# The end of a joined loop: linear products of groups 6 and 7 placed ahead of the first two key tiles, key and value weight halves cast one round earlier

## What is computed

```python
    x = x + _L0_attn_ref(_layernorm(x, axis=-1), ...)      # gated linear attention
    x = x + _L0_ffn_ref(_layernorm(x, axis=-1), ...)       # x2 and w2 rounded to a 6-bit grid, out = xd @ wd.T + bias
    x = x + _L1_xattn_ref(_layernorm(x, axis=-1), ctx_1024, ctx_1024, ...)
    # in _L1_xattn_ref, 16 heads of 32 features:
    q = _split_heads(query @ Wq + bq)
    k = _split_heads(key @ Wk + bk)
    v = _split_heads(value @ Wv + bv)
```

## Time and profile before

| | us |
|---|---|
| median of 3 runs | 1305.11 |
| lowest and highest | 1301.33, 1306.03 |
| the profiled execution | 1304.07 |
| its span | 1302.80 |
| TensorE busy | 1230.7 |
| VectorE busy | 728.5 |
| ScalarE busy | 520.5 |
| GpSimd busy | 141.2 |

### The profile page before, as it was taken

How to read it: one execution, slowest core, us unless ns; L and a number is a source line. 1 busy time by engine, 2 the same in 40 slices (tenths; PEclk the granted TensorE clock), 3 DMA queues, 4 the chain that set the end, 5 groups by cost and what they waited for, 6 DMA issues and landing times. The chain is left out here.

```text
span 1302.8 us, 25903 instructions
## 1 busy us (share of the span) xinstructions
PE 1230.7 (94%) x11069; PEld 917.0 (70%) x11069; DVE 728.5 (56%) x1602; ACT 520.5 (40%) x1032; POOL 141.2 (11%) x163
## 2 busy tenths in 40 slices
PE   6999889989959999999999999999899999999999
PEld 4565467855536777777777777776788767887887
DVE  5368386638884555454545555555585745434342
ACT  3234437543112355445444545454454332222321
POOL 2300022145540300000000000000031100000000
PEclk9999999889989999999999999999899999999999
DMA  9659600200203021000001000001400201011100
GB/s 297 255 203 398 240 1 1 73 1 1 98 17 126 36 98 35 34 34 34 34 34 34 34 34 34 34 34 34 83 1 1 73 1 33 33 33 33 65 33 33
DMA packets 49334, 88.23 MB, mean 68 GB/s; under 512 B 19210, under 2 KB 20284, under 8 KB 45124
## 3 DMA queue, kind: packets, MB, share of 16 engines
q1 hardware_dynamic: 48160, 86.01, 19.3%
q10 hardware_dynamic: 1060, 0.56, 0.2%
HBM read 65.59 MB, written 20.97 MB: 66 GB/s over the span
## 5 line engine op out<-in xcount | busy, mean ns | idle before, releaser
L1941 ACT ACTIVATE W<-W,low 128x512 f32<-128x512 f32 x128 | 91.0, 713 | 58.1 <-DVE low L1858 58.1
L1926 ACT ACTIVATE K<-bank,vecT 128x512 f32<-128x512 f32 x64 | 43.7, 688 | 166.1 <-PE bank L285 166.1
L222 POOL TENSOR_TENSOR rstd<-rstd,half_pow 128x1 f32<-128x1 f32 x48 | 31.8, 664 | 715.0 <-DVE rstd L218 715.0
L285 PE MATMUL bank<-ctxT,Wkv 128*128 128x512 f32 x384 | 96.0, 403 | 10.7 <-DVE ctxT L302 10.7
L1836 DVE TENSOR_TENSOR W<-bank,vecT 128x256 f32<-128x256 f32 x16 | 6.8, 424 | 167.2 <-PE bank L1747 167.2
L1858 DVE CUSTOM_DVE_ANT_0 W<-bank,W 128x512 f32<-128x512 f32 x128 | 80.8, 687 | 31.5 <-PE bank L1726 31.5
L285 PE MATMUL bank<-xT,wT 128*128 128x512 f32 x384 | 94.8, 396 | 0.8 <-ACT W L2764 0.5
L285 PE MATMUL bank<-woT,hR 128*128 128x512 f32 x384 | 93.2, 398 | 2.3 <-DVE woT L302 2.3
L285 PE MATMUL bank<-Wkv,Wq 128*128 128x512 f32 x384 | 93.8, 399 | 0.0
L285 PE MATMUL bank<-Wq,Wkv 128*128 128x512 f32 x384 | 93.0, 394 | 0.0
L285 PE MATMUL bank<-Wkv,ctxT 128*128 128x512 f32 x384 | 92.9, 394 | 0.0
(11 more groups left out here) (345 smaller groups left out, 2232.1 us busy)
## 6 DMA issues: line engine op xcount, KB each, us to landing
W<-ctx_turned SPq DMA_DIRECT2D x16, 1024.0 KB, 4.8
W<-in_ctx_dram SPq DMA_DIRECT2D x8, 1024.0 KB, 10.2
ctx_turned<-ctxT SPq DMA_DIRECT2D x8, 1024.0 KB, 7.6
ctx_turned<-W SPq DMA_DIRECT2D x8, 1024.0 KB, 6.7
XT<-in_ctx_dram SPq DMA_DIRECT2D x4, 1024.0 KB, 11.3
XT<-in_L_ffn_wi_dram SPq DMA_DIRECT2D x4, 1024.0 KB, 6.1
XT<-in_L_ffn_wo_dram SPq DMA_DIRECT2D x4, 1024.0 KB, 5.1
raw_own<-in_ctx_dram SPq DMA_DIRECT2D x3, 1024.0 KB, 11.2
```

The lines of the kernel that those rows point to most:

```text
L222: pool.tensor_tensor(rstd[:, g:g + 1], rstd[:, g:g + 1], half_pow[:], ALU.pow).then_inc(rstd_ok.s, 1)
L285: ins = pe.matmul(dst, stationary(x, k), moving(y, k), start=(first and n == 0), stop=(last and n == len(passes) - 1), skip_group_check=True)
L1926: act.activation(K[:, m, :], bank[:, n % 4, :], ACT.Identity, bias=pcol("L1_xattn_bk", m)).then_inc(ring_a.s, 1)
L1941: act.activation(PR[:, j, :], PR[:, j, :], ACT.Exp, bias=low[:, j:j + 1], scale=-1.0, accum_out=total[:, j:j + 1]).then_inc(expd.s, 1)
```

## The change

On TensorE, key tile 0 leaves round 12 and key tile 1 leaves its place ahead of the linear product of group 7. Both now stand at the end of round 13, behind that product. The waits for the sums of groups 6 and 7 in front of key tiles 2 and 3 become one wait for the sum of group 7 in front of the first transpose of the next stage. On ScalarE and VectorE, the key and value weight halves are made in rounds 1 to 4 in place of 2 to 5. No instruction is added or removed but the one wait.

```diff
@@ -1213,8 +1213,6 @@
                     if 1 <= t <= G:
                         mean_of_pe(t - 1)
-                    if t in (G + 4, G + 5):
-                        key_pe(t - G - 4)
                     if 6 <= t:
                         linear_pe(t - 6)
@@ -1223,6 +1221,9 @@
                     if 1 <= t <= G:
                         variance_pe(t - 1)
+                    if t == G + 5:
+                        for m in range(2):
+                            key_pe(m)
@@ -1410,8 +1411,8 @@
-                    if 2 <= t < C + 2:
-                        key_weights_v(t - 2)
+                    if 1 <= t <= C:
+                        key_weights_v(t - 1)
@@ -1577,8 +1578,8 @@
-                    if 2 <= t < C + 2:
-                        key_weights_a(t - 2)
+                    if t <= C:
+                        key_weights_a(t - 1)
@@ -1766,6 +1767,7 @@
             def tensor():
+                pe.wait_ge(xsum.s, xsum(nth("xsum", 2, G - 1)))
                 for g in range(G):
@@ -1773,7 +1775,6 @@
                     transpose_rows(xn, 3, g, 4 + g % 3)
                     if g in (2, 5):
-                        pe.wait_ge(xsum.s, xsum(nth("xsum", 2, 6 + g // 3)))
                         keys_pe(0, 2 + g // 3)
```

## The result

The changed kernel takes 1297.30 us (median of 20 runs, 1289.72 to 1305.05), the kernel before 1304.96 (20 runs, 1299.51 to 1311.16). The ratio is 0.9948, 95% interval 0.9931 to 0.9964, so the change is worth 6.8 us of 1305, with 4.7 to 9.0 in the interval; the medians are 7.7 apart. The profiled execution took 1300.68 us with a span of 1299.4.

A forecast was written before the change was run, and what follows sets the result against it. The prediction took TensorE, busy for 94% of the span, to bound the kernel. Its terms, 8.5 + 0.8 + 0.75 - 2.0 = 8.05 us off 1305.11, gave 1297.1 us, range 1293.6 to 1302.

The forecast's parts named there:

- Part 1, the order: Rounds 12 and 13 on TensorE: two linear products and one turn fill the 10.3 us idle time, gaining 8.5 us.
- the waits for half_x: On TensorE in front of transposes 3 to 5: half_x is ready earlier, so 0.8 us of waits go.
- Part 2, the new wait: In front of the eight transposes: the wait for group 7's sum costs nothing, covered by 2.6 us.
- Part 3, the weight halves: Key weight halves a round sooner shorten TensorE's 1.22 us wait in round 5: gain 0.75 us, bounds 0 and 1.2.
- Part 4, the clock: Idle gaps around the turn of group 7 take TensorE to 1.2 GHz: loss 2.0 us, bounds 0 and 4.6.
- The upper bound of 4.6: Largest clock loss in us, if TensorE's clock comes back only at 394.2, 9.2 us at half from 385.0.
- the held clock: Rival, 27%: TensorE's clock does not fall around the turn of group 7; gain 10.05 us, time 1295.1.
- the clock comes back as late as before: Rival, 18%, shared with a late VectorE chain: TensorE's clock loss 4.6 in place of 2.0, gain 5.4, time about 1300.
- something else holds the products: Rival, 7%: something else releases linear products 6 and 7, the idle time fills only partly; gain 0 to 3, time 1303.5.
- the slower one: Rival, 3%: scattered gaps from 382 hold 1.2 GHz into the query products; lasting to 440, loss 27, time 1322.
- nothing behind 416 gives the gain back: After the first query product: waits there hang on work that moves along, so no gain is lost.
- the prediction's own signs of being wrong: A wait for X before the transposes, clock 0.5 past 394, or first query product to end longer than 886.5 us.

The follow-up runs named there:

- the order alone: The kernel before with only the new TensorE order and the one wait, weight halves in rounds 2 to 5 as before: 1294.46 us (0.9931), again 1299.16 us (0.9961).
- The late sum: The changed kernel with ten useless 128x512 products on VectorE ahead of the sum of group 7; profiled once, distance from group 6's turn to the queries 36.32 us.

## Why the prediction was right

The forecast was 1297.1 us with a range of 1293.6 to 1302.0; measured is 1297.3. By its steps:

- **Part 1, the order.** Worked out at 8.5 us to the start of the transposes, plus 0.8 for the waits for half_x, 9.3 in all. With the clock held, which is the case that this term describes, the runs give 39.05 - 28.57 = 10.5 (before's first profile, from whose rows the term was worked out, against the order alone). The term was 1.2 too small for that profile; against before's second, with a key tile of 4.39 in place of 5.46 us, the gain is 9.0. Half of the 1.2 is that I laid shown durations end to end: from the start of product 7 to the transposes the order alone took 9.03 us (380.98 to 390.01) where I had 9.65 (385.7 to 395.35), 3.14 for the product and 5.89 for the two key tiles. The other half is in the transposes: from their start to the queries it is 11.0 us (397.21 to 408.19) against 12.4 before, a gain of 1.4 for which I had 0.8. Groups 3 to 5 are now one run of twelve in 1.47 us, where before had eight in 1.32, a wait, and four in 0.66. The split of the 8.5 was a little off as well: start to start, the hidden products and the turn were 7.6 us and not 7.3, the key tile's part 2.1 and not 2.4.
- **Part 2, the new wait.** Costed at nothing, and no wait for X is in the trace. The cover of 2.6 was worked out for a held clock, and the order alone has 2.4 (sum of group 7 done at 387.62, transposes at 390.01); in the changed kernel it was 4.6, since product 7 ran slow. The late sum confirmed the one-to-one loss beyond it, but there the price has a second part that I did not name, the clock.
- **Part 3, the weight halves.** 0.75 estimated, 0.78 measured in two pairs of profiles.
- **Part 4, the clock.** The fall was the forecast's case and came in all four profiles of the changed kernel. I priced it at 2.0; it is 2.95. It starts before the product of group 7, which takes 6.50 us for 3.60, and lasts 6.8 us (384.25 to 391.07), twice the 3.4 seen at 271. It fell on product 7 and not on the key tile, which therefore started at 391.34 and not near 389, and took its usual 3 us. The upper bound of 4.6 was not reached.

The two errors, a gain 1.2 too small and a loss 0.95 too small, nearly cancel: by the measured terms 10.5 + 0.8 - 2.95 = 8.3 us against the forecast's 8.05, and 8.07 at the queries, since the joined loop began 0.26 us later in the profile after. That closeness is luck; and with before's second profile the same sum is 6.9. The mechanism was right, the two sizes were not. The Trainium skill (TensorE: Matmul & The Clock Gate, Part 1: The HAM clock gate) warns of long idle gaps, but tells also of a kernel whose frequent short ones made the clock fall and rise. The changed kernel's traces agree with the second, a gap of 2.25 us followed by one of 0.68 being enough; the order alone, with the same gaps and the clock at 1.00, shows that shortness alone doesn't settle it.

Of the rivals, the held clock is real, but in other kernels' profiles. The one that the clock comes back as late as before did not happen (back near 391, not 394), nor did the one that something else holds the products, nor the slower one.

The sentence that nothing behind 416 gives the gain back is right on average (tails of 889.0 over two profiles of before, 888.2 over four of the changed kernel) and was wrong for the profile at hand: 891.2 us against 886.5 was one of the prediction's own signs of being wrong, and only the further profiles took it back. I had a spread of three runs, 4.7 us, and took 1 us of it into the range; over 20 runs the spread is 12 to 15 and the median of the kernel before still moves by 1.2 us from one series to the next, and with 10 to 12 runs that of the order alone moved by 4.7. The chance of 0.63 for faster by over 0.5% fits: the ratio is 0.9948, with the bound of 0.9950 inside its interval.

## What to carry to other kernels

Where an in-order engine waits for a late operand, look at what stands behind it in its queue and is ready already; moving that ahead is worth its full start-to-start time (3.43 us for a linear product here), and another 1.3 to 2.7 us here for key tile 0 and the product behind it, which then run at the full clock, as long as the clock holds in the new order. A product split into high and low halves has passes that need only the early half; they are the natural filler. Two short gaps close together on TensorE can cost as much in clock (2.95 us here) as in idle time (2.93), so fill the larger one even with part of a tile, and judge a gain of under 1% from distances inside several traces, since the stretch behind the change alone moved by 7 us from profile to profile here, with no difference in the code there.

## What I had not expected of the hardware

The same gaps (2.25 and 0.68 us around 0.66 us of work) left the granted clock at 1.00 in two profiles of one kernel and took it to 0.50 in four of another: 28.6 or 31.5 us for the same matmuls. The two kernels differ in where the gap lies against an earlier fall of the clock, by 0.7 to 1.1 us. In the five profiles with a fall there (the late sum's among them) it came 112.64 us behind that earlier one each time. Eight useless matmuls of 128x512 in the larger gap went with a stretch 2.94 us shorter than in the changed kernel. The 10.3 us gap of the kernel before left the first key tile at 5.46 us in one profile and at 4.39 in another.
